# Down products of each second expert pair moved one pair later, hidden activations in two buffers

## The reference, cut to what matters

```python
xn = layernorm(x)
out = x + attention(xn) + experts(xn)
# attention: 16 heads of width 16, rotary positions, causal softmax, an output projection
# experts, for each token:
scores = softmax(xn @ gate_weight.T)              # 64 experts
topk_w, topk_idx = top_k(scores, 8); topk_w /= sum(topk_w)
y = sum over its 8 experts of topk_w * ((silu(xn @ w_gate[e]) * (xn @ w_up[e])) @ w_down[e])
```

## Time and profile before

| | us |
|---|---|
| median of 3 timed runs (lowest, highest) | 454.42 (453.11, 456.04) |
| span of the profiled execution | 520.9 |
| first gate_up product of group 0 on PE | 285.23 |
| first gate_up product of group 15 on PE | 429.70 |
| start of the spill group on PE | 440.62 |

### The profile page before, as it was taken

How to read it: one execution, slowest core, us unless ns; L and a number is a source line. 1 busy time by engine, 2 the same in 40 slices (tenths; PEclk the granted TensorE clock), 3 DMA queues, 4 the chain that set the end, 5 groups by cost and what they waited for, 6 DMA issues and landing times.

```text
span 520.9 us, 6975 instructions
## 1 busy us (share of the span) xinstructions
PE 380.6 (73%) x2250; PEld 251.8 (48%) x2250; DVE 260.1 (50%) x541; ACT 170.9 (33%) x376; POOL 178.0 (34%) x204
## 2 busy tenths in 40 slices
PE   3993577632029898999998989878888886799600
PEld 1552334311015453554554868767777765564400
DVE  5776898940017656577560332332332331047498
ACT  4444200000015341555555333233233242257200
POOL 4655457777720000000000335535535536300000
PEclk9997555555558687899999998999989998599965
DMA  6268876222210007000004888778878845174150
GB/s 198 81 183 235 191 186 210 108 107 107 107 43 1 1 3 162 1 3 2 1 3 122 284 281 272 230 234 265 250 229 261 242 155 162 33 312 143 40 191 30
DMA packets 38900, 73.84 MB, mean 142 GB/s; under 512 B 7094, under 2 KB 25801, under 8 KB 37840
## 3 DMA queue, kind: packets, MB, share of 16 engines
q1 hardware_dynamic: 30192, 47.28, 32.1%
q0 software_dynamic: 8112, 25.71, 13.4%
q10 hardware_dynamic: 560, 0.41, 0.2%
HBM read 50.41 MB, written 25.05 MB: 145 GB/s over the span
## 4 chain that ended last, share of the span: by engine, by line
PE 53%; DVE 20%; another core or an unknown queue 15%; ACT 4%; issue 3%; SPq 2%; DMA 1%; POOL 1%; DVEq 0%; ACTq 0%
PE ps L1071 11%; PE ps L982 9%; PE ps L958 7%; PE ps L1004 7%; DVE rows L1493 4%; PE ps L1080 4%; DVE mx_low L1372 3%; DVE mx L1372 2%; PE ps L891 2%; ACT work L802 2%; PE ps L985 2%; PE ps L962 2%; PE ps L1087 2%; ACT probs L789 2%
## 5 line engine op out<-in xcount | busy, mean ns | idle before, releaser
L693 POOL DMA_INDIRECT rank_results<-work,dst x81 | 79.8, 985 | 224.8 <-ACT work L824 198.0
L789 ACT ACTIVATE probs<-ps 128x128 f32<-128x128 f32 (+3 forms) x192 | 85.3, 491 | 168.6 <-PE ps L985 73.0
L982 PE MATMUL ps<-qz,kz 128*128 128x128 f32 (+3 forms) x192 | 78.3, 459 | 43.7 <-ACT probs L789 35.2
L958 PE MATMUL ps<-kz,qz 96*128 96x512 f32 (+3 forms) x192 | 84.6, 512 | 20.7 <-DVE mx L1372 11.5
L1372 DVE TENSOR_REDUCE mx<-ps 128x1 f32<-128x512 f32 (+3 forms) x88 | 53.8, 638 | 64.1 <-remote 41.6
L982 PEld LDWEIGHTS ps<-qz,kz 128*128 128x128 f32 x192 | 41.3, 219 | 77.4 <-ACT probs L789 55.6
L688 POOL DMA_INDIRECT expert_rows<-rows,slot_i x64 | 63.5, 992 | 20.0 <-issue 18.4
L1421 DVE SCALAR_TENSOR_TENSOR work<-work,ps 96x320 f32<-96x320 f32 x32 | 15.5, 484 | 104.8 <-issue 64.1
L958 PEld LDWEIGHTS ps<-kz,qz 96*128 96x128 f32 x192 | 48.7, 256 | 30.3 <-DVE mx L1372 10.6
L1372 DVE TENSOR_REDUCE mx_low<-ps 128x1 f32<-128x512 f32 x64 | 41.4, 685 | 17.3 <-PE ps L958 15.7
L1004 PE MATMUL ps<-probs,v_aug 128*20 128x512 f32 (+3 forms) x384 | 43.9, 537 | 0.4 <-ACT probs L789 0.4
(11 more groups left out here) (177 smaller groups left out, 450.2 us busy)
## 6 DMA issues: line engine op xcount, KB each, us to landing
work<-rank_results POOLq DMA_DIRECT2D x8, 1024.0 KB, 5.6
gate_up_first<-w_gu SPq DMA_DIRECT2D x8, 768.0 KB
probs<-w_gu SPq DMA_DIRECT2D x8, 768.0 KB
rows<-expert_rows SPq DMA_DIRECT2D x32, 136.0 KB
probs<-expert_rows SPq DMA_DIRECT2D x32, 136.0 KB
qz<-qk_parts SPq DMA_DIRECT2D x16, 256.0 KB, 5.6
rows<-w_down SPq DMA_DIRECT2D x8, 384.0 KB
probs<-w_down SPq DMA_DIRECT2D x8, 384.0 KB
```

Of the source, the lines that this page charges most:

```text
L693: pool.indirect_dma_start(yd[:, :], bass.IndirectOffsetOnAxis(ap=at, axis=0), source, None, bounds_check=N * K - 1, oob_is_err=False).then ...
L789: act.activation(probs[:, step % 2, j, lo:hi], ps[:, B_BANKS[n % len(B_BANKS)], lo % HALF:(hi - 1) % HALF + 1], ACT.Exp, scale=DK ** -0.5) ...
L958: last = pe.matmul(bank[:, n * width:(n + 1) * width], head_rows(qz, g, j, i, 96), kz[g % SLOTS][0:96, lo // HALF, j, 0:width], start=True ...
L982: last = pe.matmul(bank[:, a:b], head_rows(kz, g, j, kt, P), qz[g % SLOTS][:, lo // HALF, j, a:b], start=True, stop=True, skip_group_check ...
```

## The change

On PE the second down product of a group (`down(n, 1)`) moves behind the first gate_up and the first transposes of the next group, and `spare_down(n)` behind the next group's second gate_up. ACT's results and DVE's order follow, and the ring of PSUM banks is dealt out in the new order. The hidden activations `hh` get a second buffer (`n % 2`), and waits that stood for the single buffer come one group later. No instruction is added or taken away, apart from one more semaphore wait in `spare_down`. After the last group `down(15, 1)` and `spare_down(15)` stand as before. SP's and POOL's programs are not touched.

```diff
@@ ring_order
-    for n in range(NG):
-        for p in range(2):
-            order += [("x", n + 1, p)] if n + 1 < NG else []
-            order += [("y", n, p)]
+    for n in range(NG + 1):
+        order += [("x", n + 1, 0)] if n + 1 < NG else []
+        order += [("y", n - 1, 1)] if n >= 1 else []
+        order += [("y", n, 0)] if n < NG else []
+        order += [("x", n + 1, 1)] if n + 1 < NG else []
@@ build
-        th, sg, hh = ([hidden_part(2 * a + p) for p in range(2)] for a in range(3))
+        th, sg, *hh = ([hidden_part(2 * a + p) for p in range(2)] for a in range(4))
@@ ScalarE, experts
                     tanh(n, 0, CAP)
-                    tanh(n, 1, CAP)
                     if n + 1 < NG:
                         xT_pair(n + 1)
+                    if n >= 1:
+                        result(n - 1, 1)
+                    tanh(n, 1, CAP)
+                    if n >= 1:
+                        spare_result(n - 1)
                     result(n, 0)
-                    result(n, 1)
-                    spare_result(n)
+                result(NG - 1, 1)
+                spare_result(NG - 1)
                 spill_group(0)
@@ TensorE, transpose_spare and spare_down
-                if n >= 2:
-                    pe.wait_ge(s_yxe, n - 1)
+                if n >= 3:
+                    pe.wait_ge(s_yxe, n - 2)
...
-                pe.wait_ge(s_Xxe, min(n + 2, NG))
+                pe.wait_ge(s_Xxe, min(n + 3, NG))
+                if n >= 1:
+                    pe.wait_ge(s_yxe, n)
@@ TensorE, experts
                     gate_up(n, 0)
-                    gate_up(n, 1)
                     if n + 1 < NG:
                         transpose_pair(n + 1, 0)
                         transpose_spare(n + 1)
+                    if n >= 1:
+                        down(n - 1, 1)
+                    gate_up(n, 1)
+                    if n >= 1:
+                        spare_down(n - 1)
                     pe.wait_ge(s_wd[n % 2], 16 * (n // 2 + 1))
                     down(n, 0)
                     if n + 1 < NG:
                         transpose_pair(n + 1, 1)
-                    down(n, 1)
-                    spare_down(n)
+                down(NG - 1, 1)
+                spare_down(NG - 1)
                 spill_group(0)
@@ VectorE, hidden and experts
-                if n >= 1:
-                    dve.wait_ge(s_dn, 2 * n + p - 1)
-                    dve.wait_ge(s_dnx, n)
+                if n >= 2:
+                    dve.wait_ge(s_dn, 2 * n + p - 3)
+                    dve.wait_ge(s_dnx, n - 1)
...
                     hidden(n, 0)
-                    hidden(n, 1)
                     if n + 1 < NG:
                         address(n + 1)
                         xT_spare(n + 1)
+                    hidden(n, 1)
+                    if n + 1 < NG:
                         xT_pair(n + 1)
```

More of the change, by code:

```diff
@@ L1079, in down @@
                 for e in range(2):
-                    last = pe.matmul(bank[:, e * D:(e + 1) * D], hh[p][:, e, 0:P],
+                    last = pe.matmul(bank[:, e * D:(e + 1) * D], hh[n % 2][p][:, e, 0:P],
                                      wdn[n % 2][0:I, (2 * p + e) * D:(2 * p + e + 1) * D], start=True, stop=True)
@@ L1084, in spare_down @@
             def spare_down(n):
-                pe.wait_ge(s_Xxe, min(n + 2, NG))
+                pe.wait_ge(s_Xxe, min(n + 3, NG))
+                if n >= 1:
+                    pe.wait_ge(s_yxe, n)
                 for e in range(EG):
-                    last = pe.matmul(ps[EXTRA * e:EXTRA * (e + 1), EXTRA_BANK, D:2 * D], hh[e // 2][:, e % 2, P:CAP],
+                    last = pe.matmul(ps[EXTRA * e:EXTRA * (e + 1), EXTRA_BANK, D:2 * D], hh[n % 2][e // 2][:, e % 2, P:CAP],
                                      wdn[n % 2][0:I, e * D:(e + 1) * D], start=True, stop=True, skip_group_check=True)
@@ L1423, in hidden @@
                 dve.wait_ge(s_sg, n * 2 + p + 1)
-                dve.tensor_tensor(hh[p][:, :, :], sg[p][:, :, :], bank[:, :, CAP:2 * CAP], ALU.mult).then_inc(s_h, 1)
+                dve.tensor_tensor(hh[n % 2][p][:, :, :], sg[p][:, :, :], bank[:, :, CAP:2 * CAP], ALU.mult).then_inc(s_h, 1)
             def xT_pair(n):
```

## The result

| | before | after |
|---|---|---|
| median of 4 runs each (lowest, highest), us | 454.15 (453.11, 456.04) | 462.71 (459.35, 467.08) |
| ratio after / before, 95% interval | | 1.0218 [1.0156, 1.0281] |
| span of the profiled execution, us | 520.9 | 465.3 |

The change makes the kernel slower, by 2.2% or 9.9 us (454.15 x 0.0218).

What follows compares the result with a forecast made beforehand. Timed expert groups were taken as about 7.88 us, all PE's work, without stalls to remove. Only the later spill loads counted, every other term being 0: 454.4 + 4.4 = 458.8 us, range 442 to 466.

Steps and rivals of the forecast that it cites:

- Late completions: News of PE's finished matmuls comes late under the profiler, promptly in timed runs; a timed group takes about 7.88 us.
- 499: Span in us forecast for a profiled execution after the change: 520.9 - 14 x 1.88 + 4.4.
- the 46 us of the earlier trace: From 94 to 154 us, 46.0 us of waits on an unknown releaser, read as late completions and kept in the profiled-span forecast.
- PE's order, price 0: In expert groups of 7.88 us without a stall, moving a down product later saves nothing in the timed runs.
- The end, +4.4: After group 14, the spill group's loads start 4.4 us later, with little PE work left to hide them: +4.4 us.
- Rows, price 0: SP's row and weight loads still arrive in time, though transposes need the rows some 3.7 us earlier: price 0.
- 5 for the last spare rows: Time in us left from issue to need of a group's last spare rows, counted in PE's new order.
- Transfers late: Rival, slower: slack of load_down or the rows gone, a 0.5 us wait in 14 groups, 466 us; chance 0.08.
- Late completions belong to the chip: Rival, faster: timed runs have the experts' late completions too; 432 to 433 us, 446 with half the lateness; chance 0.17.
- Small cover: Rival: tanh or hidden slightly later than in group 0, about 3 us over 15 groups now hidden; 455.8 us; chance 0.15.
- PE's clock: Rival, slower: clock stays 2.4 GHz before and falls only after, ahead of the spill group; 459.5 to 464 us; chance 0.18.

Runs made afterwards that it cites:

- c0: The kernel before, unchanged, run and profiled once more: 454.89 us, ratio to before 0.9975.
- c3: The changed kernel with the old order at both ends of the experts (groups 0 and 1, and group 14's down products): 452.00 us, ratio to before 1.0000.
- c2: The changed kernel with the old order at the start only (groups 0 and 1): 461.32 us, ratio to before 1.0225.
- c1: The changed kernel with the old order at the end only (group 14's down and spare_down stay in group 14): 460.58 us, ratio to before 1.0168.
- d4: The changed kernel with group 2's rows and the spill group's gate/up weights and rows both loaded early: 453.61 us, ratio to before 1.0064.
- d3: The changed kernel with group 2's rows issued ahead of SP's wait for group 0's gate_up: 458.67 us, ratio to before 1.0137.
- f2: c2 plus 38 idle products on PE in the wait ahead of the spill group: 454.46 us, ratio to before 1.0103.
- f1: The kernel before plus 13 idle products on PE in the wait ahead of the spill group: 451.09 us, ratio to before 1.0010.
- d1: The kernel before with the spill group's gate/up weights and rows loaded early: 449.79 us, ratio to before 0.9948.
- h1: The kernel before with group 2's rows and the spill group's gate/up weights and rows both loaded early: 444.48 us, ratio to before 0.9877.

## Why the prediction was right, and where not

**The sign and the size.** 458.8 was forecast within 442 to 466, with slower as the likeliest; 462.71 was measured. The mechanism of the forecast holds, and a second one, somewhat larger, was priced at 0. That the time still lies in the range is luck in part: the room up to 466 was left for the rivals, and none of them had the loss at the start.

**Late completions.** The conclusion, that timed groups take about 7.9 us and that the change has no stall to remove there, was right (c0: 7.91; c3: 1.0000). The reason, "under the profiler", was wrong: c0 and all later profiles are without it, and the timed runs are profiled too. So the profiled span did not come out at 499 but at 465.3: the 46 us of the earlier trace rows that the working left in were gone as well. What made PE's news late in that execution stays open; POOL's indirect DMAs alone are not enough, as they are in every profile.

**PE's order, price 0.** Right: 7.94 against 7.91 us a group, and a cover of 3.2 us that nothing uses.

**The end, +4.4.** Right in place and size: the first spill load behind group 15's second gate_up, 8.22 us of idle PE ("about 8"), 2.99 before ("about 3"), released by the row load; 4.45 us in the traces. c2 shows that this end alone makes it slower.

**Rows, price 0: the step that failed.** "The eight row loads keep their place" was true of SP's program, and the slack, "5 for the last spare rows", holds for groups 2 to 14 of after: no wait for rows or weights there. (It is small: with the new order in the middle groups, c1, c3 and d4 do have waits for rows there, 0.1 to 1.0 us each.) It was counted in the steady state and used for all. In groups 0 and 1 the lead is not there yet: group 1's rows are issued when group 0 already begins, and group 2's stand behind the wait for group 0's second gate_up, which the new order puts 2.5 us later, counted from the beginning of group 0, while it wants the rows 2 us sooner. That makes 4.83 us of waits for 1.19, and behind them some 3 us at a clock of 0.50, in which PE's work takes 1.8 us longer than elsewhere: together about the 5.6 us. The rival "Transfers late" came nearest, with a chance of 0.08, but spread the waits over 14 groups, 0.5 us each, and looked for a limit of bandwidth, where it is one of order on SP's queue: d3 takes the 2.79 us away by issuing the same rows earlier, with no byte less.

**The other rivals.** *Late completions belong to the chip* (faster): refuted by c0. *Small cover* (a gain of 3 us): refuted by c0, whose groups 2 to 14 take 7.91 us each, and by c3. *PE's clock*: c2's 10.2 us is 5.7 more than the end's 4.45, about the 5 that the rival adds, though its trace has only 1 us of it (5.4); and f2 shows that the clock falls for want of work in the longer wait and gets half of c2's loss back. The Trainium skill (TensorE: Matmul & The Clock Gate, "What's actually happening") has an idle PE throttled to 1.2 GHz; f2 agrees, 1.00 with idle products against 0.59 without. But the rival's condition, that before keeps the clock there, is not seen: in c0 and after alike the stretch from spill to attention takes 11.1 us at 0.50. Only the timed ratios speak for it (f1 shows no gain, f2 does), so its share stays open.

## What to carry to other kernels

A software pipeline that is shifted by a step is priced three times: in the steady state, in its first groups, where the loads have not yet got their lead, and in its last, where the next stage's loads hang on the shifted step. For each load ask behind which wait its issue stands, and whether the shift moves that wait; here two sets of loads issued earlier on SP's queue gave 1.2% on the unshifted kernel, and the shift, with both its ends put back, nothing that could be measured. A profile whose span is far above the timed runs is taken again before any of its waits is explained.

## What the runs showed of the hardware

One execution of an unchanged kernel took 66 us longer than the next (520.9 and 454.5). By the working before the result the news of its matmuls came up to 2 us late in the experts, and later still from 94 to 154 us; what caused it is not shown, and it did not come back in 13 further profiles of these kernels. Of the clock: in c0 it fell in a wait of 3.0 us, and in after behind waits of 2.79 and 0.60 us and again in the wait of 8.2 us; from that one it stays at 0.50 through the whole spill group, with PE at work again from 385.00, and comes back only in the attention, after 400. In f2 it was held through the wait and fell to 0.50 all the same at 379, as PE began to stand for 2.79 us between the spill group and the attention. The length of the wait alone doesn't set when it falls: d1 and h1 both wait 0.77 us ahead of the spill group, but h1 runs all of it at 0.50 (11.06 us), and d1 keeps 1.00 until 373.5, 2 us into it (9.84 us).
